# DLRM bilinear tower, head of the first chunk: pieces of weights and next indices issued at other times, landing waits of the first gathers lagged by one group

## The chip, the core and the metric

The kernel runs on one NeuronCore of a Trainium2 chip. The metric is the device time of one execution in microseconds (us). It is the median of several runs; a profile shows one execution with every instruction of every engine. The engines are TensorE (PE, with its weight loads PEld), VectorE (DVE), ScalarE (ACT), GpSimd (POOL) and SyncE (SP, which here only issues DMAs).

## What is computed

40 embedding tables are looked up for 2048 rows of a batch. Every pair of fields then gives one bilinear number, and the 780 numbers and 16 dense features go through three layers:

```python
e = jnp.stack([tbl_f[ids[:, f]] for f in range(40)], axis=1)      # (2048, 40, 64)
rowidx, colidx = pair_indices(40)                                   # 780 pairs i < j
z = jnp.einsum('bie,fie,bif->bi', e[:, rowidx], param, e[:, colidx])
h = jnp.concatenate([z, dense_ctx], axis=1)
h = jnp.maximum(h @ W_top1 + b_top1, 0.0)                           # 796 -> 512
h = jnp.maximum(h @ W_top2 + b_top2, 0.0)                           # 512 -> 256
y = h @ W_top3                                                      # 256 -> 1
```

All is float32. (`stack` and `pair_indices` are abridged here.)

## The kernel before

**Tiling.** The batch is cut into four chunks of 512 rows. Two fields make a tile, so a chunk has 20 tiles. A tile is needed in transposed form `e_t` (128 = 2 fields of 64 values, by 512 batch rows), and tiles 0 to 3 of a chunk also in the gathered form `rows` (batch rows on partitions).

**Getting a tile.** GpSimd gathers table rows with indirect DMAs (L481). One gather fetches 128 rows of one field, so a tile takes two groups of four gathers, one group for each field. TensorE then transposes the tile by four matmuls with an identity (L701), and ScalarE copies it out of PSUM into `e_t` (L502). In the first chunk only, tiles 4 to 7 (small tables) come another way: their tables are loaded whole by SyncE (L431), VectorE writes one-hots (L647), and TensorE multiplies them with the tables (L690, `look_up_tile`).

**The items.** The pairs are worked off as a list of items in a fixed order, the same for all engines. A "unit" (m, k) is two matmuls (L727) whose results VectorE multiplies into `prod` (L606, L603); sums of eight such blocks, a group, are then formed by TensorE with a strip of ones (L750, `sum_group`). VectorE may only write a slot of `prod` again (12 units) once its group is summed. A "wide" item is two matmuls (L732) for tile m against the fixed tiles 0 to 3; VectorE multiplies (L619), and ScalarE adds up the products (L541, 32 instructions each), or VectorE for some of them (L630).

**Order in the head of the first chunk.** TensorE looks up tiles 4 and 5, does the units of row 5, tile 6, the units of row 6, tile 7, the units of row 7, then transposes tiles 0 and 1, does the two units of row 1, transposes tile 2, the two units of row 2, transposes tile 3, unit (3,0), a group sum, units (3,1) to (3,3), a group sum, and from there the wide items of rows 4, 5, 6 and so on, four to a row. The transpose of tile 8 comes right before the wide items of row 6 (`TILES_AT`, items 16 and 24). Later chunks repeat the pattern without lookups, with the tiles prepared a chunk ahead.

**Weights.** The bilinear matrices come in pieces of 12 columns of 128 (768 KB), in three slots (`w`, `W_SLOTS`). SyncE issues them in one program-ordered queue: indices of chunk 0, the small tables and piece 0 between them; then it waits until tile 0 is transposed (the wait before `load_idx(1)`), issues the indices of chunk 1 and pieces 1 and 2; and from piece 3 on it waits each time until the last item that reads the piece three before is done (`t_ready`). Piece 0 holds the units of rows 5 to 7 and of rows 1 and 2, piece 1 those of row 3 and the wide items of rows 4 and 5, piece 2 the wide items of rows 6, 7 and 8. Hence piece 3 waits for row 2's last unit.

**GpSimd's queue.** It works off the tiles in the order 0 to 3, 8, 9 and so on. After each group of four gathers it waits until this group has landed, except behind the very first group. One semaphore for each slot of `rows` counts both fields. The slots are eight for the fixed tiles and six for the others. The landing wait is:

```python
if c > 0 or m > 0 or f > 0:
    pool.wait_ge(gathered[slot], 16 * BT * (f + 1 + 2 * (use - 1)))
```

TensorE's `transpose_tile` waits for the same semaphore at the count of both fields.

## Time and profile before

| what | us |
|---|---|
| median of 3 runs | 1275.88 |
| lowest and highest run | 1272.23, 1280.07 |
| profiled execution | 1274.63 |
| span of its core, first to last instruction | 1272.8 |
| TensorE busy | 1231.0 |
| VectorE busy | 1023.4 |
| ScalarE busy | 1023.9 |
| GpSimd busy | 577.7 |

The span is what the trace covers; the profiled execution's own time is 1.8 us longer. Times in the trace count from the span's start. In a row of a timeline the first number is the start, the second the length of the merged piece, and the bracket holds the idle time of the engine before it and what ended that. Busy times of matmuls overlap, since they are pipelined. "Issue" is idle time in which the engine waited for nothing that the profile shows.

### The profile page before, as it was taken

Reading aid. Unit: us, or ns where it says so; the run is one execution under the profiler, and the core shown is the slowest. Engines: PE = TensorE matmul, PEld = TensorE weight load, DVE = VectorE, ACT = ScalarE, POOL = GpSimd, SP = SyncE. Lnnn points to the kernel's source line nnn. Section 1 sums busy time; section 2 is a strip of 40 time slices with the busy share of each in tenths; the row PEclk is TensorE's granted clock in tenths of the full one; section 3 lists DMA queues with packets and bytes.
Section 4 is the critical chain, followed back from the end, with each engine's and each line's share of the span. In section 5 each row is a group of like instructions: output and inputs, shape, how many; then the busy total and the mean of one; then the engine's idle time right before and its main releaser. Section 6 shows DMA issues by size and latency. Waiting matters only on the chain.

```text
span 1272.8 us, 23705 instructions
## 1 busy us (share of the span) xinstructions
PE 1231.0 (97%) x6064; PEld 481.1 (38%) x6064; DVE 1023.4 (80%) x1680; ACT 1023.9 (80%) x7945; POOL 577.7 (45%) x615
## 2 busy tenths in 40 slices
PE   6788999999999999999999999999999999999999
PEld 3233433333333343333344333433343333343333
DVE  5768999998887777888787887788889787788980
ACT  0049988777488989998958999899968898999981
POOL 5555555555555555555345555555225554000000
PEclk9989999999999999999999999999999999999999
DMA  6311422132221222222221222122112122111100
GB/s 173 94 46 46 143 72 70 45 94 64 71 70 48 70 71 70 49 67 64 66 67 47 73 69 71 45 70 72 54 59 69 46 70 67 30 47 50 44 2 0
DMA packets 33201, 80.88 MB, mean 64 GB/s; under 512 B 11773, under 2 KB 12285, under 8 KB 32937
## 3 DMA queue, kind: packets, MB, share of 16 engines
q1 hardware_dynamic: 12320, 57.17, 13.9%
q0 software_dynamic: 19456, 19.96, 7.7%
q10 hardware_dynamic: 1288, 2.24, 0.6%
q8 instruction: 48, 0.79, 0.3%
q14 instruction: 89, 0.72, 0.2%
HBM read 79.32 MB, written 0.01 MB: 62 GB/s over the span
## 4 chain that ended last, share of the span: by engine, by line
PE 60%; ACT 31%; issue 3%; DMA 2%; POOL 2%; DVE 1%; another core or an unknown queue 1%; ACTq 0%
ACT wide_prod L541 29%; PE ring L727 26%; PE z_ps L750 13%; PE ring L732 11%; PE ring L756 7%; DMA rows<-tbl,idx_now 2%; POOL rows L481 2%; PE ring L701 2%; ACT e_t L502 1%; PE ring L760 1%; DMA idx_now<-idx 0%; DVE prod L606 0%; PE ring L763 0%; PE ring L708 0%
## 5 line engine op out<-in xcount | busy, mean ns | idle before, releaser
L541 ACT ACTIVATE wide_prod<-wide_prod 128x64 f32<-128x64 f32 x3904 | 933.7, 243 | 52.4 <-DVE wide_prod L619 25.6
L481 POOL DMA_INDIRECT rows<-tbl,idx_now x608 | 576.9, 949 | 496.7 <-DMA rows<-tbl,idx_now 292.2
L541 ACT ACTIVATION_READ_ACCUMULATOR wide_prod<-wide_prod 128x1 f32 x3904 | 739.4, 189 | 24.4 <-issue 23.4
L606 DVE TENSOR_TENSOR prod<-ring,e_t 128x512 f32<-128x512 f32 x1008 | 630.8, 683 | 147.6 <-PE ring L727 101.1
L727 PE MATMUL ring<-e_t,w 64*128 64x512 f32 x2176 | 563.0, 609 | 9.6 <-ACT e_t L502 5.9
L619 DVE TENSOR_TENSOR wide_prod<-ring,rows 128x512 f32<-128x512 f32 x512 | 328.3, 682 | 44.6 <-PE ring L732 33.3
L727 PEld LDWEIGHTS ring<-e_t,w 64*128 64x128 f32 x2176 | 215.9, 187 | 300.1 <-issue 203.7
L732 PE MATMUL ring<-w,e_t 64*128 64x512 f32 x1024 | 292.1, 607 | 11.4 <-ACT e_t L502 7.1
L750 PE MATMUL z_ps<-prod,strip 128*32 128x512 f32 x2096 | 256.2, 603 | 0.1
L732 PEld LDWEIGHTS ring<-w,e_t 64*128 64x128 f32 x1024 | 106.2, 186 | 147.0 <-issue 86.7
L750 PEld LDWEIGHTS z_ps<-prod,strip 128*32 128x32 f32 x2096 | 55.3, 109 | 182.0 <-issue 119.6
L502 ACT ACTIVATE e_t<-ring 128x512 f32<-128x512 f32 x80 | 44.7, 587 | 90.7 <-PE ring L701 47.9
L756 PE MATMUL ring<-z_t,w 128*128 128x512 f32 x224 | 99.8, 598 | 0.0
L756 PEld LDWEIGHTS ring<-z_t,w 128*128 128x128 f32 x224 | 41.4, 190 | 56.8 <-issue 49.2
L603 DVE TENSOR_TENSOR prod<-ring,e_t 64x512 f32<-64x512 f32 x80 | 54.8, 685 | 6.2 <-PE ring L727 3.9
L701 PE MATMUL ring<-ident,rows 128*128 128x128 f32 x304 | 45.5, 284 | 7.8 <-DMA rows<-tbl,idx_now 7.8
L701 PEld LDWEIGHTS ring<-ident,rows 128*128 128x128 f32 x304 | 32.5, 142 | 49.8 <-issue 41.2
L514 ACT ACTIVATE z_t<-z_ps 128x512 f32<-128x512 f32 x20 | 11.8, 588 | 38.8 <-PE z_ps L750 30.1
L690 PE MATMUL ring<-wide_prod,z_t 125*64 125x512 f32 x128 | 30.5, 631 | 10.7 <-DMA z_t<-tbl 10.7
L550 ACT ACTIVATE h<-ring,b 128x512 f32<-128x512 f32 x16 | 10.9, 683 | 27.9 <-PE ring L756 27.8
L647 DVE TENSOR_SCALAR wide_prod<-h,first_row_f 125x512 f32<-125x512 int32 x48 | 20.4, 490 | 12.1 <-DMA z_t<-tbl 8.3
L760 PE MATMUL ring<-h,w 128*128 128x512 f32 x64 | 29.2, 602 | 0.0
(23 smaller groups left out, 79.3 us busy)
## 6 DMA issues: line engine op xcount, KB each, us to landing
w<-weights SPq DMA_DIRECT2D x64, 768.0 KB
rows<-tbl,idx_now POOLq DMA_INDIRECT x608
w<-weights SPq DMA_DIRECT2D x4, 512.0 KB
z_t<-tbl SPq DMA_DIRECT2D x8, 224.0 KB
w<-w1z SPq DMA_DIRECT2D x1, 1792.0 KB
h<-hot_ids ACTq DMA_DIRECT2D x6, 256.0 KB
z_t<-hot_ids ACTq DMA_DIRECT2D x2, 256.0 KB
w<-w2p SPq DMA_DIRECT2D x1, 512.0 KB
```

Source lines behind the costliest of these rows:

```text
L481: nc.gpsimd.indirect_dma_start(out=rows[:, slot, t, E * f:E * f + E], out_offset=None, in_=tables[m * 2 + f], in_offset=bass.IndirectOffse ...
L502: nc.scalar.activation(e_t[:, m, :], ring[:, BANKS["tile", tile][0], :], ACT.Copy).then_inc(e_ready, 1)
L541: last = nc.scalar.activation(products, products, ACT.Copy, accum_out=z_b[:, h, t, col:col + 1])
L603: nc.vector.tensor_tensor(dst[half, 0, :], ring[half, bank, :], e_t[half, m - 1 + j, :], ALU.mult).then_inc(t_free, 1)
L606: nc.vector.tensor_tensor(dst[:, j, :], ring[:, bank, :], e_t[:, k, :], ALU.mult).then_inc(t_free, 1)
L619: nc.vector.tensor_tensor(dst[:, j, :, :], src[:, bank, :, :], rows[:, fixed_slot(c):fixed_slot(c) + FIXED, t, :], ALU.mult).then_inc(t_fr ...
L701: last = nc.tensor.transpose(dst[:, P * t:P * t + P], rows[:, slot, t, :], ident[:, :])
L727: nc.tensor.matmul(dst, w[field, slot, P * o:P * o + P], e_t[field, m - 1 if diagonal and b == 0 else m, :], start=True, stop=True).then_i ...
L732: nc.tensor.matmul(dst, e_t[field, m, P * t:P * t + P], w[field, slot, P * o:P * o + FIXED * P], start=True, stop=True).then_inc(t_ready, 1)
L750: last = nc.tensor.matmul(z_ps[32 * col:32 * col + 32, :], strip[:, 30 - 2 * r:62 - 2 * r], prod[:, (c * NU + UNIT_PLACE[c][u]) % PROD_SLO ...
L756: return nc.tensor.matmul(dst, w1[:, t * H1 + P * h:t * H1 + P * h + P], z_t[:, Z_NUMBER[c, t] % Z_SLOTS, :], start=start, stop=stop)
L760: return nc.tensor.matmul(dst, w2[:, k, P * h:P * h + P], h1[:, k, :], start=k == 0, stop=k == KH1 - 1)
```

## The change

Only the schedule is changed, at four places:

- SyncE issues piece 1 as soon as both fields of tile 0 have landed. Then it waits until tile 3 is transposed, issues piece 2 and after it the indices of chunk 1. Before, all three went out once tile 0 was transposed, the indices first.
- Each slot of `rows` has two semaphores, one for each field.
- For the first four tiles (the first eight groups of gathers) GpSimd waits, after it has issued a group, for the group before it. For all other tiles it waits for the group just issued, as before. The last group of tile 3 is thus waited for by nobody on GpSimd.
- TensorE waits for two semaphores instead of one before each transposed tile.

```diff
--- before.py
+++ after.py
@@ -383,7 +383,7 @@
         strip_written = sem("strip_written")
         idx_in = sem("idx_in")
         mlp_in = sem("mlp_in")
-        gathered = [sem(f"gathered{i}") for i in range(2 * FIXED + G_SLOTS)]
+        gathered = [[sem(f"gathered{i}_{f}") for f in range(2)] for i in range(2 * FIXED + G_SLOTS)]
         w_in = [sem(f"w_in{i}") for i in range(W_SLOTS)]
         dense_in = sem("dense_in")
         hot_in = [sem(f"hot_in{i}") for i in range(len(ONE_HOT))]
@@ -437,10 +437,12 @@
             for i in range(2, len(ONE_HOT)):
                 load_tables(i)
 
-            sp.wait_ge(transposed, T_NUMBER[0] + 1)
+            for f in range(2):
+                sp.wait_ge(gathered[fixed_slot(0)][f], 16 * BT)
+            load(1)
+            sp.wait_ge(transposed, T_NUMBER[FIXED - 1] + 1)
+            load(2)
             load_idx(1)
-            for piece in range(1, W_SLOTS):
-                load(piece)
             for piece in range(W_SLOTS, len(PIECES)):
 
                 sp.wait_ge(t_ready, through(PIECES[piece - W_SLOTS][2]))
@@ -463,6 +465,7 @@
                                     base=0, pattern=[[-1, P]], channel_multiplier=1).then_inc(consts, 1)
             nc.gpsimd.iota(first_row[:, :], [[1, 1]], base=0, channel_multiplier=HOT_J).then_inc(rows_known, 1)
             pool.wait_ge(idx_in, 16)
+            under_way = None
             for tile in GATHERED:
                 c, m = divmod(tile, TILES)
                 slot, use = slot_of(tile)
@@ -481,10 +484,16 @@
                         nc.gpsimd.indirect_dma_start(
                             out=rows[:, slot, t, E * f:E * f + E], out_offset=None, in_=tables[m * 2 + f],
                             in_offset=bass.IndirectOffsetOnAxis(ap=idx_now[:, c % 2, col:col + 1], axis=0),
-                        ).then_inc(gathered[slot], 16)
-                    if c > 0 or m > 0 or f > 0:
-
-                        pool.wait_ge(gathered[slot], 16 * BT * (f + 1 + 2 * (use - 1)))
+                        ).then_inc(gathered[slot][f], 16)
+                    landed = gathered[slot][f], 16 * BT * use
+                    if c == 0 and m < FIXED:
+
+                        if under_way is not None:
+                            pool.wait_ge(*under_way)
+                        under_way = landed
+                    else:
+
+                        pool.wait_ge(*landed)
 
         @block.scalar
         def _(act):
@@ -695,7 +704,8 @@
 
             def transpose_tile(tile):
                 slot, use = slot_of(tile)
-                pe.wait_ge(gathered[slot], use * 2 * BT * 16)
+                for f in range(2):
+                    pe.wait_ge(gathered[slot][f], use * BT * 16)
                 dst = take_bank(("tile", tile))
                 for t in range(BT):
                     last = nc.tensor.transpose(dst[:, P * t:P * t + P], rows[:, slot, t, :], ident[:, :])
```

## Rows read from the trace of the kernel before

**Rows 1.** The page: busy time by engine; granted clock in 40 slices of the span

```profile
PE 1231.0 (97%) x6064; PEld 481.1 (38%) x6064; DVE 1023.4 (80%) x1680; ACT 1023.9 (80%) x7945; POOL 577.7 (45%) x615
...
PEclk9989999999999999999999999999999999999999
```

**Rows 2.** Waits of TensorE, whole run: line and what it waited for, us, times, longest

```profile
PE ring L701 <- DMA rows<-tbl,idx_now: 7.8, 1, 7.8
...
PE ring L727 <- issue: 1.7, 3, 1.1
```

**Rows 3.** The chain in order of time, 60 to 84 us: start, us, what

```profile
63.18 2.44 DMA rows<-tbl,idx_now
...
80.20 3.83 ACT wide_prod L541 x31
```

**Rows 4.** The same chain, 100 to 260 us

```profile
167.18 1.13 PE ring L727 x4
```

**Rows 5.** Timeline of GpSimd: start, us, instruction, idle before and what ended it

```profile
4.92 1.11 POOL L481 DMA_INDIRECT rows<-tbl,idx_now  x1 [3.37 <-DMA idx_now<-idx]
...
14.56 1.15 POOL L481 DMA_INDIRECT rows<-tbl,idx_now  x1 [0.31 <-issue]
21.54 1.02 POOL L481 DMA_INDIRECT rows<-tbl,idx_now  x1 [5.83 <-DMA rows<-tbl,idx_now]
...
25.70 1.32 POOL L481 DMA_INDIRECT rows<-tbl,idx_now  x1 [0.30 <-issue]
28.75 0.94 POOL L481 DMA_INDIRECT rows<-tbl,idx_now  x1 [1.73 <-DMA rows<-tbl,idx_now]
...
53.05 0.94 POOL L481 DMA_INDIRECT rows<-tbl,idx_now  x1 [0.30 <-issue]
59.44 0.94 POOL L481 DMA_INDIRECT rows<-tbl,idx_now  x1 [5.45 <-DMA rows<-tbl,idx_now]
```

**Rows 6.** Timeline of SyncE's DMA issues, 50 to 60 us

```profile
51.86 6.40 SPq L421 DMA_DIRECT2D w<-weights  x3
```

**Rows 7.** The gathers' DMA queue, 4 to 15 us: packets, MB, share

```profile
q0 software_dynamic: 132, 0.14, 4.6%
```

**Rows 8.** Groups of instructions by line, GpSimd, 16 to 57.87 us

```profile
L481 POOL DMA_INDIRECT rows<-tbl,idx_now x20 | 21.1, 1055 | 17.2 <-DMA rows<-tbl,idx_now 12.6 <-issue 4.6
```

**Rows 9.** Timeline of TensorE, 50 to 90 us

```profile
54.53 0.66 PE L701 MATMUL ring<-ident,rows 128*128 128x128 f32 x4
55.88 1.99 PE L727 MATMUL ring<-e_t,w 64*128 64x512 f32 x8 [0.69 <-ACT e_t L502]
65.67 1.12 PE L701 MATMUL ring<-ident,rows 128*128 128x128 f32 x4 [7.80 <-DMA rows<-tbl,idx_now]
67.47 2.08 PE L727 MATMUL ring<-e_t,w 64*128 64x512 f32 x4 [0.69 <-ACT e_t L502]
69.47 3.64 PE L750 MATMUL z_ps<-prod,strip 128*32 128x512 f32 x16
73.05 2.89 PE L727 MATMUL ring<-e_t,w 64*128 64x512 f32 x12
75.87 1.92 PE L750 MATMUL z_ps<-prod,strip 128*32 128x512 f32 x16
77.72 3.70 PE L732 MATMUL ring<-w,e_t 64*128 64x512 f32 x16
...
87.95 2.39 PE L732 MATMUL ring<-w,e_t 64*128 64x512 f32 x7 [0.45 <-issue]
```

**Rows 10.** Stretches: us; PE, PEld, DVE, ACT, POOL busy; granted clock, DMA share, GB/s

```profile
50.00:57.87 7.87, 6.44 (x32) 2.68 (x30) 6.68 (x12) 1.68 (x3) 3.08 (x4) 1.00 0.67 224
57.87:65.67 7.80, 0.01 (x1) 0.01 (x1) 1.65 (x3) 0.00 (x0) 3.77 (x4) 0.82 0.41 121
65.67:73.05 7.38, 6.69 (x25) 1.81 (x25) 0.00 (x0) 0.60 (x1) 4.41 (x5) 0.50 0.10 20
```

**Rows 11.** Groups of instructions by line, VectorE's one-hots, 21.6 to 26.9 us

```profile
L647 DVE TENSOR_SCALAR wide_prod<-h,first_row_f 125x512 f32<-125x512 int32 x14 | 6.1, 495 | 0.0
```

## The prediction, made before the changed kernel was run

> **What bounds the kernel now.** I read the page first: TensorE is busy for 1231.0 us, 97% of the span, and only the first slices of the span show less, with the granted clock dipping in the third [rows 1]. So the body is bound by TensorE's own work, and the head is the place where time is idle. The waits of TensorE over the whole run put a number on that: one single wait of 7.80 us of the transpose at L701 for a gather's landing [rows 2]. The only longer one, before the first lookup, is untouched by this change.
>
> The chain of waits says where that stall sits. Up to 65.62 us it runs through GpSimd's gathers and their landing, then through the transposes of tile 3, units, group sums, and the first wide items; from 80.20 us it is ScalarE's reduction of the wide products [rows 3]. ScalarE sets the pace until 167 us, where the chain changes to TensorE and stays there [rows 4]. Nothing in that chain after 65.67 us waits for a transfer. Both stages are orders of instructions, written out, whose waits are on each other. If the first wide item starts x us sooner, ScalarE starts x sooner, and TensorE takes over x sooner.
>
> **Why tile 3 is late.** GpSimd issues eight groups of four gathers for tiles 0 to 3 (two fields each). It stops after every group but the first until that group has landed [rows 5]. The gathers begin at 4.92 us. Groups 1 and 2 are issued without a stop, by 14.56 + 1.15 = 15.71. Then GpSimd idles 5.83 us for group 2, behind the tables and the first piece. The usual stop is 1.7 us (1.73 before 28.75; four of this kind). The stop before the last group is 5.45 us, because its predecessor was issued up to 53.99 while SyncE's loads of pieces 1, 2 and 3 went out from 51.86 [rows 5, 6]. The last group starts at 59.44, is issued by 64.12 and has landed by 65.62 [rows 3, 5]: 1.5 us after.
>
> **The change, part by part.**
>
> *Waits lag by four gathers.* Group n+1 is issued while group n lands. At most eight gathers are open at a time, as already at the head now. When does group 3 start? Group 1 needs 4 x 32 = 128 packets of the gathers' queue, and 132 had moved by 15 us [rows 7]. So its landing is over at about 15.7, and group 3 starts near 16.0, where it now starts at 21.54. Groups 3 to 8 are 24 gathers. The 20 started between 16 and 57.87 had a mean of 1.055 us, with 0.30 between gathers [rows 8]. So 24 x 1.355 = 32.5 us: issued by 48.5, landed by 50.0. The bound on the slow side takes the longest gather of the head, 1.32 us [rows 5], for all of them, since more will now lie beside VectorE's one-hots: 24 x 1.62 = 38.9, issued by 54.9, landed by 56.4. If group 3 does not start before 21.54 but the rest holds: 21.54 + 32.5 + 1.5 = 55.5. TensorE is ready for tile 3 at 57.87 (its last unit of the row starts at 55.88 and ends 1.99 later [rows 9]). In each of these three the stall is gone; with both handicaps, 21.54 + 38.9 + 1.5 = 61.9, and 4.1 us of it stay.
>
> Tile 2 is transposed at 54.53 us, and tiles 0 and 1 before it, without a wait now, and the gathers only get earlier, so nothing is won there. The lookups before them do not use the gathers.
>
> The Trainium skill (SBUF — State Buffer, the section with the two separate sides) has a rule against this part: VectorE in a two-port mode and GpSimd hold a shared port pair exclusively, and the later one is blocked for the whole instruction. The head's longer gathers beside one-hots fit it, but no more than 1.32 - 0.94 = 0.38 us is seen of it.
>
> *Piece 1 at about 21.3 us instead of 51.9.* SyncE waits for both groups of tile 0, which end where GpSimd's wait now ends. It meets groups 3 and 4. Three pieces made one stop 5.45 - 1.7 = 3.75 us longer, so one piece costs a landing at most as much. That is 1.7 + 3.75 = 5.45 after issue, and the next group takes 4 x 1.355 = 5.4 to issue, so GpSimd waits for nothing or 0.1 us. TensorE needs piece 1 at unit (3,0), right behind tile 3: no cost. Without the cover of the lag it would be 3.75 us once, and tile 3 landed at 53.8 for 50.0, still in time.
>
> *Piece 2 and the next indices behind tile 3's transposes.* These run at about 58.5, and SyncE then issues piece 2, the indices (chunk 1's, needed beyond 200 us) and piece 3, whose condition (piece 0 read, 57.9) holds. Now three pieces, issued from 51.86, are in before 65.67, where the transfers drop to 21 GB/s [rows 6, 10]: 13.8 us at most, so all is in by 72.3. Piece 2 is first read by the wide item of row 6, at 87.95 now [rows 9] and 77.0 after: 4.7 us to spare at the least. The loads meet the gathers of tile 8, transposed just before that item; GpSimd is by then at least as far ahead of today as TensorE. The cost is nothing.
>
> *Two semaphores a slot, and one more wait before each of 76 transposed tiles.* The trace shows no such row. From below it is nothing: TensorE already waits for a bank before every matmul of a unit, more than a thousand times, and its idle time put down to issue before them is 1.7 us in all [rows 2]. From above, the gap between two gathers on GpSimd, 0.30 us [rows 5], would make 22.8 us. TensorE's own row is the nearer one: under 2 ns each, so I take 0.1 us.
>
> *The slow clock goes with the stall.* The granted clock is full from 50 to 57.87, has a mean of 0.82 in the idle stretch and is 0.50 (1.2 GHz) from 65.67 to 73.05 [rows 10]. What ran there at half rate, against its like at the full one [rows 9]: transposes and copy of tile 3 65.67 to 67.47 = 1.80 against 54.53 to 55.88 = 1.35; unit (3,0) 67.47 to 69.47 = 2.00 against a third of 73.05 to 75.87, 0.94; first group sum 69.47 to 73.05 = 3.58 against 75.87 to 77.72 = 1.85. Together 0.45 + 1.06 + 1.73 = 3.24 us. The Trainium skill (TensorE: Matmul & The Clock Gate, Part 1) has the same two levels, idle and busy; the row agrees.
>
> **Sum.** 7.80 + 3.24 - 0.1 = 10.9 us. The first wide item then starts at 57.87 + 1.35 + 0.94 + 1.85 + 2.82 + 1.85 = 66.7 instead of 77.72. The profiled execution took 1274.63 us around a span of 1272.8; it becomes 1263.7 around 1261.9. The three runs have their median 1.25 us higher, at 1275.88, so the forecast is 1275.88 - 10.9 = 1265.0, 0.85% faster.
>
> **Rivals.**
> - *Tile 3 still late.* Gathers beside one-hots grow, or the early piece delays groups 3 and 4. For it: the 5.83 us stop at 15.7 and gathers of 1.32 us; against it: room of 1.5 us or more by each single bound. With both handicaps 4.1 us stay, so 1269.1; with the clock falling too, 1272.3. A gather lengthened by one whole one-hot of 0.495 us [rows 11] each time would be 0.94 + 0.50 + 0.30 = 1.74, 24 of them 41.8, landed by 59.3, 1.4 us late: 1266.4. That is what the rule of the Trainium skill's page SBUF — State Buffer would make of it. Chance 0.10.
> - *The clock falls without the stall*, because of the short waits for ScalarE's copies there (0.69 us). Only 7.8 us come: 1268.1. Against it: 1.00 through a wait of the same 0.69 us before 55.88 [rows 9, 10]. Chance 0.05.
> - *No change.* The gain is eaten where ScalarE bounds, if something fixed in time holds the wide items: piece 2, or tile 8. Against it: the room worked out above. 1275.9. Chance 0.05.
> - *Slower.* The second wait before a transpose is not hidden, at 0.30 us for each of 76 tiles: 22.8 - 11.0, so 1287.7. It decides the sign from 11.0 / 76 = 0.145 us on. Against it: TensorE's small issue time. Chance 0.04.
> - *As forecast*: 0.76.
>
> **How the numbers follow.** A measurement of this kernel can tell about 1%, 12.8 us, from no change. The three runs before lie 7.8 us apart, so the likeliest case's own range is 1265 ± 4, 1261 to 1269. On the slow side the range takes in most of the late tile, to 1271; on the fast side a microsecond more: 1260 to 1271. Faster by over 1% needs 1263.1 or less, 1.9 us under the forecast: well within that spread, some 0.37 of the likeliest case, 0.28. Slower by over 1% is the slower rival and a little: 0.05. Within 1%: 0.67.
>
> **What would show it.** Right: GpSimd's third group starts near 16 us and the eighth is issued by 48 to 55; no wait of L701 for a gather; granted clock 1.00 from 50 to 80 us; the first wide matmul near 66.7, ScalarE's first reduction near 69.2, the change of the chain to TensorE near 156; span 1262. Piece 1 issued near 21.4, piece 2 near 58.5. Wrong: idle time of TensorE before L701 or before L732's row 6; issue gaps before transposes in the body; a stretch at 0.50 between 55 and 75 us.

## The result and the profile after

The changed kernel takes 1300.85 us in the median of six runs (1286.22 to 1303.63); the kernel before took 1274.82 beside it (six runs, 1272.23 to 1280.07). The ratio is 1.0171, with a 95% interval of 1.014 to 1.0202: slower by 1.7%, where 0.85% faster was forecast. The profiled execution is the fastest of the six, 1286.22 us around a span of 1284.4 (1272.8 before), so the trace can show only 11.6 of some 26 us.

Lines of the new kernel: gathers L484, lookups L699, transposes L711, units L737, wide items L742, group sums L760, copies into `e_t` L511, reductions L550, one-hots L656.

First the page, against [rows 1]: 9.5 us more of TensorE's busy time, and a third slice that is no better.

```profile
PE 1240.5 (97%) x6064; PEld 485.4 (38%) x6064; DVE 1023.6 (80%) x1680; ACT 1023.9 (80%) x7945; POOL 580.1 (45%) x615
...
PEclk9889999999999999999999999999999999999999
```

GpSimd's timeline, against [rows 5]. It does what the change says: the third group starts at 15.69 (before 21.54), without a stop, and the eighth, the last of tile 3, is issued by 50.20 + 0.94 = 51.14. The last landing on record for it is at 52.42; before, it had landed at 65.62 [rows 3]. The row at 55.20 is the last gather of tile 8's first group, the ninth. GpSimd does wait for that one, 1.77 us, up to 57.91.

```profile
15.69 0.94 POOL L484 DMA_INDIRECT rows<-tbl,idx_now  x1 [0.30 <-issue]
...
21.81 0.94 POOL L484 DMA_INDIRECT rows<-tbl,idx_now  x1 [1.31 <-DMA rows<-tbl,idx_now]
...
26.19 3.66 POOL L484 DMA_INDIRECT rows<-tbl,idx_now  x1 [0.30 <-issue]
...
50.20 0.94 POOL L484 DMA_INDIRECT rows<-tbl,idx_now  x1 [0.30 <-issue]
...
55.20 0.94 POOL L484 DMA_INDIRECT rows<-tbl,idx_now  x1 [0.30 <-issue]
57.91 0.94 POOL L484 DMA_INDIRECT rows<-tbl,idx_now  x1 [1.77 <-DMA rows<-tbl,idx_now]
```

TensorE's timeline, against [rows 9]. The wait of 7.80 us for a gather is gone: tile 3 is transposed at 77.61 with no idle time before it. But there is a new wait of 9.59 us, put down to issue, before the units of row 7. The first wide item starts at 86.52; before it was 77.72, and 66.7 was forecast.

```profile
46.46 2.50 PE L699 MATMUL ring<-wide_prod,z_t 125*64 125x512 f32 x6 [0.34 <-issue]
50.21 1.07 PE L699 MATMUL ring<-wide_prod,z_t 125*64 125x512 f32 x2 [1.24 <-DVE wide_prod L656]
60.87 5.27 PE L737 MATMUL ring<-e_t,w 64*128 64x512 f32 x16 [9.59 <-issue]
...
69.60 2.56 PE L737 MATMUL ring<-e_t,w 64*128 64x512 f32 x8 [2.44 <-issue]
...
77.61 0.69 PE L711 MATMUL ring<-ident,rows 128*128 128x128 f32 x4
...
86.52 3.70 PE L742 MATMUL ring<-w,e_t 64*128 64x512 f32 x16
```

What do the units of row 7 wait for? ScalarE's copy of tile 7. Its row in ScalarE's timeline, and two rows of the waits of the whole run (us, times, longest):

```profile
60.22 0.60 ACT L511 ACTIVATE e_t<-ring 128x512 f32<-128x512 f32 x1 [21.86 <-remote]
```

```profile
ACT wide_prod L550 <- issue: 47.0, 106, 1.0
ACT e_t L511 <- remote: 46.9, 6, 21.9
```

TensorE's last matmul of tile 7 had ended at 51.28 us, ScalarE was idle, and the copy starts 8.9 us later. "Remote" says that the profile finds no instruction ending when the semaphore rose. The trace also records when each semaphore is incremented. Here the one that TensorE increments at the end of matmuls which read a one-hot (VectorE's one-hots wait for it), and the one for a finished tile:

```
changed kernel, us from the span's start
 matmuls ended     41.40 41.40 42.26 42.26 43.11 43.12 43.97 43.98 44.83 44.84 45.69 46.12 47.53 47.93 48.97
 increments        41.62       43.04 43.09 44.48       45.90 45.94 47.33 49.46 50.20 52.36 55.23 57.34 58.74 58.78 59.46
 tile 7: ended 51.28, increment 60.19
kernel before
 matmuls ended     40.41 40.42 41.27 41.28 42.13 42.13 42.99 42.99 43.84 43.85 44.70 44.71 45.56 45.57 46.42
 increments        40.43 40.47 41.28 41.33 42.14 42.19 43.00 43.04 43.86 43.90 44.72 44.76 45.58 45.62 46.43
```

Before, every increment is there 0.01 to 0.06 us after its matmul. Now they trail further and further, by 2 us at 48 and 10 at 59 (some increments are not recorded one by one). At first one, or two at once, come each 1.4 us, where the matmuls end in pairs 0.86 us apart. Nothing in the program had touched them: increments sent by TensorE arrive late while GpSimd issues gather after gather. They are slowed, not stopped, and a stop does not let them all out: in GpSimd's stop from 56.14 to 57.91 a single one comes.

In TensorE's start times against those before, matmul by matmul, this makes +4.4 us by 50 us and +13.7 at 60.9. The clock is at half in two stretches, one around the wait of 9.59 us and one behind the wait of 2.44 us (windows: PE, PEld, DVE, ACT, POOL busy; clock; DMA share; GB/s):

```profile
53.80:64.10 10.30, 3.23 (x8) 1.53 (x10) 1.12 (x2) 0.60 (x1) 5.67 (x6) 0.50 0.13 23
...
70.90:77.70 6.80, 6.11 (x17) 1.99 (x14) 3.81 (x6) 0.60 (x1) 4.25 (x5) 0.50 0.09 19
```

With them it is +18.5 at 74.9 and +19.3 at the last unit of row 2, at 76.6. Then the old stall and its slow clock fall out, 10.5 us in all. The wide items start with +8.8, and the end comes at +11.6.

### The profile page after: what moved, and what is told of

Read it like the earlier page. It is cut to its first block, busy times and chain, and to the rows that moved or that the text cites. A ratio compares the mean times of both kernels' runs of the same rounds, so it can differ in the third digit from the quotient of the medians.

```text
span 1284.4 us, 23706 instructions
## 1 busy us (share of the span) xinstructions
PE 1240.5 (97%) x6064; PEld 485.4 (38%) x6064; DVE 1023.6 (80%) x1680; ACT 1023.9 (80%) x7945; POOL 580.1 (45%) x615
## 4 chain that ended last, share of the span: by engine, by line
PE 81%; ACT 13%; issue 3%; DVE 1%; DMA 1%; another core or an unknown queue 1%; SPq 0%; ACTq 0%; DVEq 0%
PE ring L737 35%; PE z_ps L760 17%; PE ring L742 15%; ACT wide_prod L550 12%; PE ring L766 7%; PE ring L711 2%; PE ring L770 2%; PE ring L699 2%; DVE prod L615 1%; ACT e_t L511 1%; DMA z_t<-tbl 1%; PE ring L773 0%; PE ring L718 0%; DVE wide_prod L628 0%
## 5 line engine op out<-in xcount | busy, mean ns | idle before, releaser
L550 ACT ACTIVATE wide_prod<-wide_prod 128x64 f32<-128x64 f32 x3904 | 933.6, 242 | 53.1 <-issue 24.9
L484 POOL DMA_INDIRECT rows<-tbl,idx_now x608 | 579.3, 953 | 503.2 <-DMA rows<-tbl,idx_now 275.0
L550 ACT ACTIVATION_READ_ACCUMULATOR wide_prod<-wide_prod 128x1 f32 x3904 | 736.7, 189 | 22.7 <-issue 22.2
L737 PE MATMUL ring<-e_t,w 64*128 64x512 f32 x2176 | 570.4, 611 | 22.3 <-issue 13.7
L737 PEld LDWEIGHTS ring<-e_t,w 64*128 64x128 f32 x2176 | 218.5, 187 | 316.8 <-issue 209.3
L742 PE MATMUL ring<-w,e_t 64*128 64x512 f32 x1024 | 295.2, 606 | 6.7 <-DVE wide_prod L628 2.7
L760 PE MATMUL z_ps<-prod,strip 128*32 128x512 f32 x2096 | 253.9, 598 | 0.0
L742 PEld LDWEIGHTS ring<-w,e_t 64*128 64x128 f32 x1024 | 108.3, 186 | 142.4 <-issue 86.6
L511 ACT ACTIVATE e_t<-ring 128x512 f32<-128x512 f32 x80 | 44.8, 586 | 106.6 <-remote 46.9
L760 PEld LDWEIGHTS z_ps<-prod,strip 128*32 128x32 f32 x2096 | 55.0, 109 | 179.1 <-issue 114.7
L711 PEld LDWEIGHTS ring<-ident,rows 128*128 128x128 f32 x304 | 32.6, 142 | 43.3 <-issue 43.3
L699 PE MATMUL ring<-wide_prod,z_t 125*64 125x512 f32 x128 | 33.3, 640 | 12.7 <-issue 11.4
L711 PE MATMUL ring<-ident,rows 128*128 128x128 f32 x304 | 45.5, 285 | 0.0
L559 ACT ACTIVATE h<-ring,b 128x512 f32<-128x512 f32 x16 | 10.9, 680 | 26.3 <-PE ring L766 26.1
L656 DVE TENSOR_SCALAR wide_prod<-h,first_row_f 125x512 f32<-125x512 int32 x48 | 20.6, 494 | 13.0 <-DMA z_t<-tbl 8.5
```

The lines of the kernel that those rows point to most:

```text
L484: nc.gpsimd.indirect_dma_start(out=rows[:, slot, t, E * f:E * f + E], out_offset=None, in_=tables[m * 2 + f], in_offset=bass.IndirectOffse ...
L511: nc.scalar.activation(e_t[:, m, :], ring[:, BANKS["tile", tile][0], :], ACT.Copy).then_inc(e_ready, 1)
L550: last = nc.scalar.activation(products, products, ACT.Copy, accum_out=z_b[:, h, t, col:col + 1])
L699: last = nc.tensor.matmul(dst[E * h:E * h + E, :], hot_table[2 * i + h][:, E * j:E * j + E], hot[number % len(hot)], start=j == 0, stop=j ...
L711: last = nc.tensor.transpose(dst[:, P * t:P * t + P], rows[:, slot, t, :], ident[:, :])
L737: nc.tensor.matmul(dst, w[field, slot, P * o:P * o + P], e_t[field, m - 1 if diagonal and b == 0 else m, :], start=True, stop=True).then_i ...
```

## Experiments

All ratios are to the kernel before, run on the same chip beside it. A line "Measured" gives the kernel's median in us, the median of the kernel before where it is the first of its chip, then the ratio and in brackets its 95% interval. The edits shown are shortened to the lines that matter.

### Which part does it?

`e1_again` is the changed kernel, unchanged. `e1_lag` has the two semaphores and the lag, with SyncE's queue as before. `e1_sp` has the two semaphores and SyncE's new queue, with the landing waits as before. `e1_sems` has the semaphores alone. Against the changed kernel:

```diff
# e1_lag: SyncE as before
-            for f in range(2):
-                sp.wait_ge(gathered[fixed_slot(0)][f], 16 * BT)
-            load(1)
-            sp.wait_ge(transposed, T_NUMBER[FIXED - 1] + 1)
-            load(2)
+            sp.wait_ge(transposed, T_NUMBER[0] + 1)
             load_idx(1)
+            for piece in range(1, W_SLOTS):
+                load(piece)
# e1_sp: no lag
-                    if c == 0 and m < FIXED:
-
-                        if under_way is not None:
-                            pool.wait_ge(*under_way)
-                        under_way = landed
-                    else:
+                    if c > 0 or m > 0 or f > 0:
```

> The changed kernel as it is, once more. All theories expect 1286 to 1304 us again, as its six executions so far. The question is what its trace looks like in an execution near 1300 us: theory M (increments of TensorE's semaphores arrive late while GpSimd keeps up to eight gathers open) expects more or longer stretches like the one from 51.3 to 60.2 us, where the transposed tile 7 was announced 8.9 us after TensorE's last matmul, and all of them before some 60 us, while the lag lasts. Theory B (the body itself is slower, for a cause that has nothing to do with the head) expects the head like the one seen and 15 us more behind 100 us.

Measured: 1235.94 against 1247.29, ratio 0.9933 (0.9909 to 0.9958).

> Two semaphores a slot and the lagged landing waits, but SyncE's queue as before. Theory M: the lag alone does it, so the loss is all here: 1286 to 1305 us, lookups with late increments between 16 and 60 us. Theory P (the early load of piece 1, or SyncE's wait for a gather's semaphore, does it): about 1264 us, as was forecast for the whole change, or up to 1268 with the three pieces meeting the gathers. Theory S (two semaphores and the second wait): slow here too, 1286 or more.

Measured: 1233.09, 0.9909 (0.9877 to 0.9941).

> Two semaphores a slot and SyncE's queue as in the change, but the landing waits as before. Theory M: no late increments; the stop of 5.45 us before the last group becomes 1.7, one earlier stop grows by up to that much, so tile 3 comes 0 to 3.75 us sooner: 1271 to 1276 us. Theory P: slow, 1286 or more. Theory S: slow, 1286 or more.

Measured: 1246.83, 1.0012 (0.9994 to 1.0031).

> Only the second semaphore of each slot and TensorE's second wait before a transposed tile; SyncE's queue and the landing waits as before. Theories M and P: no difference to the kernel before, 1272 to 1278 us. Theory S: all the loss is here, 1286 to 1304 us, with 0.15 to 0.4 us for each of 76 transposes, or late increments in the head without any lag.

Measured: 1247.55, 1.0003 (0.9977 to 1.0029).

This was another chip than the first, and on it the same two kernels came out the other way round: 1247 for the kernel before and not 1275, and the change faster, not slower. Four chips of this study ran the kernel before at 1247 to 1249 us (the first kind below); the first chip and three more at 1264 to 1275 (the second kind). Only one chip was measured twice, 15 minutes apart, and it was of the first kind both times. So "kind of chip" is the reading that fits; a state that a chip passes through is not excluded.

On the first kind the forecast mechanism is there. TensorE's timeline of `e1_sems`, then of `e1_again`:

```profile
55.60 1.99 PE L730 MATMUL ring<-e_t,w 64*128 64x512 f32 x8 [0.69 <-ACT e_t L504]
64.57 1.09 PE L704 MATMUL ring<-ident,rows 128*128 128x128 f32 x4 [6.98 <-issue]
...
76.83 3.70 PE L735 MATMUL ring<-w,e_t 64*128 64x512 f32 x16
...
354.83 0.66 PE L704 MATMUL ring<-ident,rows 128*128 128x128 f32 x4
367.63 1.09 PE L704 MATMUL ring<-ident,rows 128*128 128x128 f32 x4 [12.14 <-issue]
```

```profile
56.07 1.99 PE L737 MATMUL ring<-e_t,w 64*128 64x512 f32 x8 [0.69 <-ACT e_t L511]
57.99 0.66 PE L711 MATMUL ring<-ident,rows 128*128 128x128 f32 x4
...
66.87 3.70 PE L742 MATMUL ring<-w,e_t 64*128 64x512 f32 x16
...
345.05 0.66 PE L711 MATMUL ring<-ident,rows 128*128 128x128 f32 x4
351.79 1.09 PE L711 MATMUL ring<-ident,rows 128*128 128x128 f32 x4 [6.09 <-issue]
```

The stall of 6.98 us is gone, the clock is 1.00 from 50 to 80 us, and the first wide item starts at 66.87, 9.96 us earlier (66.7 was forecast). The rows near 350 us show what was not forecast: TensorE catches up with GpSimd there and waits 12.14 us for a tile of the second chunk. With GpSimd ahead from the head on, by 15.3 us at the start of the eighth group (43.11 against 58.38), 6.09 remain, so the whole gain at the end of these two traces is 16.1 us. SyncE's part and the second semaphore are worth nothing that can be measured; on this kind the lag is all of it.

### Does the half clock cost what the rows said, and is GpSimd the bound at 350 us?

`e4_filler` is the kernel before with eight more matmuls (their result is overwritten) in the stall before tile 3. They stand before the wait for the gathers, and so does the wait for the tile's bank now. This keeps the stall and takes the slow clock away. `e4_lag` repeats `e1_lag` beside it.

```diff
+                dst = take_bank(("tile", tile))
+                if tile == FIXED - 1:
+                    for _ in range(FILLERS):
+                        nc.tensor.matmul(dst, ident[:, :], e_t[:, 0, :], start=True, stop=True)
                 pe.wait_ge(gathered[slot], use * 2 * BT * 16)
-                dst = take_bank(("tile", tile))
```

> The kernel before, with eight more matmuls (identity by a tile, 128 columns by 512, 0.86 us each, 6.9 us in all, results overwritten) put on TensorE in the stall before tile 3's transposes, so that it waits without being idle. Theory C (the stretch at half clock comes from the idle time): the granted clock stays full, tile 3 is not sooner, and 2.6 us are won, as much as the offset between the traces of the change and of the kernel with only two semaphores grew behind the stall: ratio 0.998. Rival: the clock falls anyway or the extra matmuls reach beyond the landing: no gain, ratio 1.000 to 1.001. What it does not win of the change's gain is the stall itself.

Measured: 1249.12 against 1248.59, 1.0012 (0.9993 to 1.0032).

> Two semaphores a slot and the lagged waits, SyncE's queue as before, with more rounds. Where the kernel before takes 1247 us: if SyncE's part is worth nothing once the waits lag, a ratio of 0.988 to 0.991, as the change itself had on three jobs (0.9933, 0.9894, 0.9876); if it is worth the collision's 3.75 us, 0.991 to 0.994. Where the kernel before takes 1275 us: 1.015 or more if the lag is the trigger of the late increments, 0.992 if it is SyncE's part.

Measured: 1232.81, 0.9885 (0.9853 to 0.9916).

Two rows of windows, first 64.57 to 71.90 us of `e1_sems`, then the stall of `e4_filler` (PE, PEld, DVE, ACT, POOL busy; clock; DMA share; GB/s), and the rows of its TensorE that show where the gain went:

```profile
64.57:71.90 7.33, 6.64 (x24) 1.79 (x24) 0.00 (x0) 0.60 (x1) 4.60 (x5) 0.50 0.10 20
```

```profile
57.50:64.70 7.20, 7.14 (x18) 2.96 (x16) 1.73 (x3) 0.00 (x0) 3.77 (x4) 1.00 0.43 129
```

```profile
73.61 3.70 PE L736 MATMUL ring<-w,e_t 64*128 64x512 f32 x16
...
361.31 0.66 PE L705 MATMUL ring<-ident,rows 128*128 128x128 f32 x4
368.28 1.09 PE L705 MATMUL ring<-ident,rows 128*128 128x128 f32 x4 [6.32 <-DMA rows<-tbl,idx_now]
```

With the clock kept at full, the first wide item starts at 73.61 and not at 76.83: 3.22 us, where the prediction had 3.24. None of it reaches the end. The tile that TensorE needs next at 350 us is there at 368.28 against 367.63, whatever TensorE did in the head: GpSimd had not been moved. On this kind of chip only what brings GpSimd forward brings the end forward.

### More lag, on the first kind

`e2_lagall` is the change with the lag for every tile; `e3_lagall_only` has that lag with SyncE's queue as before; `e2_lag8` waits for the group before the last (twelve gathers open) in the first four tiles. `e2_again` and `e3_again` are the changed kernel beside them.

```diff
# e2_lagall
-                    if c == 0 and m < FIXED:
-
-                        if under_way is not None:
-                            pool.wait_ge(*under_way)
-                        under_way = landed
-                    else:
-
-                        pool.wait_ge(*landed)
+                    if under_way is not None:
+                        pool.wait_ge(*under_way)
+                    under_way = landed
# e2_lag8
-                        if under_way is not None:
-                            pool.wait_ge(*under_way)
-                        under_way = landed
+                        if under_way is not None and len(under_way) == 2:
+                            pool.wait_ge(*under_way.pop(0))
+                        under_way = (under_way or []) + [landed]
```

> The changed kernel once more. Two chips have given two answers: 1275 us before and 1301 after on the first, 1247 before and 1236 after on the second. Theory K (it is the chip): on a chip where the kernel before takes about 1275 us, and where ScalarE's reductions show gaps of 0.3 to 1 us after each landing of gathers, the change costs some 20 us, through late increments in the head; on a chip at about 1247 us, without these gaps, it gains 11 us. Theory N (it was a passing state of the first chip or job): the gain is there whatever the kernel before takes.

Measured: 1232.78 against 1247.25, 0.9894 (0.9854 to 0.9934).

> The changed kernel with the lagged landing wait for every tile, not only the first four. On a chip at 1247 us before: the last stall of TensorE for a gather (6.1 us at 346 to 352 us in the trace of the change, 12.1 before) goes with its stretch at half clock, so 8 us more than the change: about 1228 us; if that stall is not GpSimd's lateness but a transfer's own time, 1236 as the change. On a chip at 1275 us before, theory K with late increments for as long as eight gathers are open: far slower, 1330 us or more, since it lasts for the whole run; theory N: about 1255.

Measured: 1224.38, 0.9831 (0.9789 to 0.9874).

> The changed kernel with the landing wait of the first four tiles lagged by eight gathers, so up to twelve open. On a chip at 1247 us before: tile 3 was in time already with a lag of four, only the stop of 0.5 us at 20.9 goes, so 1236 as the change, and at most 1 us better at tile 28. On a chip at 1275 us before, theory K: the more gathers are open, the later the increments, so slower than the change by some us, 1305 to 1315; if the number open does not matter, 1301.

Measured: 1231.94, 0.9895 (0.9853 to 0.9938).

> The changed kernel on whatever chip comes. Theory K: about 1235 us where the kernel before takes 1247 and its trace keeps all 16 landing increments of each gather; about 1300 us where the kernel before takes 1275 and increments are missing from the trace, with TensorE's increments in the head late. Theory N: a gain of some 11 us in either case.

Measured: 1232.78 against 1249.37, 0.9876 (0.9855 to 0.9897).

> Landing waits lagged by four gathers for every tile, SyncE's queue as in the kernel before. If the moved loads of pieces 1 and 2 bring nothing of the gain: 1224 us at 1247 before, as with them. If they do bring something once the waits lag, the three pieces meeting the gathers at 52 us cost a part of the head's gain: 1228 us. On a chip with 1275 us before, theory K and the lag as its trigger: slower than the change, over 1310 us; if it is SyncE's part that triggers it, under 1265.

Measured: 1224.63, 0.9809 (0.9788 to 0.983).

Lag by one group is enough in the head; the lag everywhere takes the rest of the stall at 350 us too (in `e2_lagall` the pair of transposes runs at 345.14 without a wait) and gives the two fastest kernels here, 1.7 to 1.9% faster than the one before. So far this reads as a success.

### The second kind: one stop less, SyncE's queue, and the lag with a pause

`e5_pairs` (SyncE as before) issues both groups of a tile and then waits for both: eight gathers open as with the lag, but GpSimd stops after each eight. `e5_sp` is `e1_sp`. `e6_lag` is `e1_lag`. `e6_breath` is `e1_lag` with four small memsets on GpSimd after each group of the first four tiles, each waited for, a pause of 1.8 to 2.4 us from the end of a group to the next gather.

```diff
# e5_pairs
-                        if under_way is not None:
-                            pool.wait_ge(*under_way)
-                        under_way = landed
+                        if f == 1:
+                            pool.wait_ge(gathered[slot][0], 16 * BT)
+                            pool.wait_ge(*landed)
# e6_breath
+                        for _ in range(BREATHS):
+                            breaths += 1
+                            nc.gpsimd.memset(scratch[:, :], 0.0).then_inc(breath, 1)
+                            pool.wait_ge(breath, breaths)
                         if under_way is not None:
```

> Two semaphores a slot, SyncE's queue as before; for the first four tiles GpSimd waits once a tile, for both its fields, instead of once a field. So up to eight gathers open as with the lag, but four stops. Theory G (at 1247 us before: the end goes by GpSimd's time, since TensorE waits for it again near 350 us): the stops after the first field of tiles 1 to 3 go, of 1.7, 1.7 and 1.7 us or a little more, so GpSimd is 5 to 6 us earlier, TensorE's stall near 350 us is 5 to 6 us shorter, ratio 0.995 to 0.997. Theory T (the end goes by TensorE's head alone): the head's stall of 7.0 us shrinks by the same 5 and the clock may stay: 0.993. Where the kernel before takes 1275 us: if more than four open gathers are the trigger of the late increments, 1.01 or more; if it is GpSimd never waiting, 0.995.

Measured: 1269.25 against 1273.38, 0.9978 (0.9953 to 1.0003).

> SyncE's queue as in the change, two semaphores a slot, landing waits as before, as once already (ratio 1.0012, 0.9994 to 1.0031). Where the kernel before takes 1247 us: the same, 1.000 to 1.003. Where it takes 1275 us: 1.015 or more if SyncE's part is the trigger of the loss there, about 1.000 if the lag is.

Measured: 1273.50, 1.0011 (0.9991 to 1.0032).

> Two semaphores a slot and the lagged waits, SyncE's queue as before. Where the kernel before takes 1273 to 1275 us and its trace has gaps in ScalarE's reductions (the slow kind of chip; SyncE's part alone gave 1.0011 there): theory K with the lag as the trigger says 1.013 to 1.02 and late increments of TensorE in the head; if it takes lag and moved loads together, 0.99 to 0.995. Where the kernel before takes 1247 us: 0.9885 to 0.991 once more.

Measured: 1269.33 (1256.35 to 1278.32) against 1263.73, 1.0022 (0.9988 to 1.0055).

> The lag without SyncE's part, and after each of the first eight groups four small memsets on GpSimd, each waited for: a pause of 1 to 3 us without any gather's landing being waited for. On the fast kind: theory G says that GpSimd's time is the end's time, so eight pauses cost the 8 to 20 us that GpSimd loses, up to the point where tile 3 is late again; the eighth group would be issued by 56 to 68 instead of 54.5 us, and the ratio is 0.995 to 1.003 instead of 0.989. On the slow kind: if gathers without a pause are what holds TensorE's increments back, they are in time again and the ratio is 0.99 to 1.00; if it is that no landing is waited for, it stays at 1.015.

Measured: 1264.08, 1.0008 (0.9989 to 1.0028). The eighth group is issued by 61.61 us here and by 48.51 in `e1_lag`; the 54.5 of the expectation is near the end of the ninth there.

`e5_sp` clears SyncE's part alone here too. TensorE's timeline of `e6_lag` and then of `e6_breath`:

```profile
29.96 7.09 PE L697 MATMUL ring<-wide_prod,z_t 125*64 125x512 f32 x32
43.59 3.78 PE L735 MATMUL ring<-e_t,w 64*128 64x512 f32 x8 [6.55 <-issue]
...
64.83 6.35 PE L735 MATMUL ring<-e_t,w 64*128 64x512 f32 x16 [3.16 <-issue]
...
87.01 3.27 PE L740 MATMUL ring<-w,e_t 64*128 64x512 f32 x14
```

```profile
37.76 1.99 PE L743 MATMUL ring<-e_t,w 64*128 64x512 f32 x8 [0.72 <-ACT e_t L517]
...
47.48 3.70 PE L743 MATMUL ring<-e_t,w 64*128 64x512 f32 x16 [0.72 <-issue]
...
75.00 3.70 PE L748 MATMUL ring<-w,e_t 64*128 64x512 f32 x16
```

ScalarE's copies of tiles 6 and 7 in `e6_lag`, then its copy of tile 2 in `e5_pairs`:

```profile
42.94 0.60 ACT L509 ACTIVATE e_t<-ring 128x512 f32<-128x512 f32 x1 [14.96 <-remote]
64.18 0.60 ACT L509 ACTIVATE e_t<-ring 128x512 f32<-128x512 f32 x1 [20.64 <-remote]
```

```profile
57.12 0.60 ACT L509 ACTIVATE e_t<-ring 128x512 f32<-128x512 f32 x1 [4.73 <-remote]
```

The lag alone brings the late increments back, without SyncE's part: the copies of tiles 6 and 7 start 5.9 and 2.5 us after everything they need has ended (37.04 and 61.67 us), and the first wide item is at 87.01. The same kernel on the first kind had no late copy. With the pause no copy in the head is late, at the same eight open gathers, and the first wide item is 12 us earlier. In `e5_pairs` one copy in the head is 2.1 us late. So it is not the number of open gathers.

Is it the missing stops, or only the faster pace of the gathers? `e6_breath` does not tell: its 24 gathers of groups 3 to 8 take 42.5 us from start to end, as long as in the kernel before (42.6). `e5_pairs` does in part: 35.0 us, the pace of the changed kernel (35.5), with a stop after each eight gathers, and its latest copy is 2.1 us late and not 8.9. That speaks for the stops, over two chips and one trace of each.

In time the lag alone did not do what either theory said: 1.0022, where the lag as the only trigger was to cost 1.3 to 2%. On this chip it was even with the kernel before, although its first wide item is as late as the changed kernel's. It is 12.0 us behind `e6_breath` there and 7.3 at the end of the traces, and in the ratios the two cannot be told apart. The changed kernel was 1.7% slower on the first chip. How much of that is the lag's alone, how much needs SyncE's loads beside it, and how much is the chip or the single execution, no run separates.

`e7_breath1`, with one memset a group, was to find the smallest pause that helps, beside `e7_again`, the changed kernel. The chip turned out to be of the first kind, so it could only say that the small pause costs nothing there.

> The changed kernel on whatever chip comes, after one chip (8, 11, 5) kind at 1247 us and three at 1264 to 1275. Where the kernel before takes 1260 us or more: ratio 1.002 to 1.02, with late increments of TensorE between 16 and 65 us in the trace, as on the first chip and as the lag alone showed at 1264. Where it takes 1247: 0.988 to 0.993, none late.

Measured: 1233.58 against 1248.50, 0.9906 (0.9876 to 0.9937).

> The lag without SyncE's part, with one small memset of GpSimd a group instead of four: a pause of some 0.8 instead of 2.4 us. Where the kernel before takes 1260 us or more: if any pause lets the held increments out, they are in time, tile 3 lands near 57 us and the ratio is 0.990 to 0.997; if the length of the pause matters, some are late and it is 1.000 or more. Where it takes 1247 us: theory G, GpSimd 8 x 0.5 us later than with the lag alone: ratio 0.991 to 0.994.

Measured: 1233.77, 0.9892 (0.9858 to 0.9926).

### The dose: the lag for every tile, on the second kind

`e8_lagall_only` is `e3_lagall_only`, to the letter. If gathers issued back to back are the cause, then more of them must hold TensorE back more.

> The lag of four gathers for every tile, SyncE's order as before; on chips of the first kind it ran at 0.981 of the kernel before. Theory A (gathers issued back to back, with no stop of GpSimd, hold back TensorE's increments, but only on a chip of the second kind, on which the kernel before takes 1264 to 1275 us): on such a chip TensorE's copies of tiles 6 and 7 are 3 us late or more in the head, TensorE is behind by 10 us at 70 us, and further late increments show wherever GpSimd runs without a stop in the body; ratio 1.00 to 1.04. Rival B (the loss in the head does not matter, since on either kind the end is set by GpSimd near 350 us): ratio 0.98 to 0.985 on either kind. If the chip is of the first kind (before at 1247), both say 0.981 again, and the second kind stays open for this kernel.

Measured: 1800.60 us (1792.63 to 1805.35) against 1275.35, ratio 1.4134 (1.4093 to 1.4174). One of the two fastest kernels of the first kind is by 41% the slowest of the second. Theory A has the direction right, and its own number, 1.00 to 1.04, is far too small. GpSimd's, TensorE's, ScalarE's and VectorE's timelines of `e8_lagall_only`, and the windows 48 to 88 us and the last 180 us:

```profile
55.68 0.95 POOL L482 DMA_INDIRECT rows<-tbl,idx_now  x1 [0.30 <-issue]
56.94 0.95 POOL L482 DMA_INDIRECT rows<-tbl,idx_now  x1 [0.30 <-issue]
```

```profile
47.08 1.59 PE L692 MATMUL ring<-wide_prod,z_t 125*64 125x512 f32 x2 [1.04 <-issue]
87.90 3.79 PE L730 MATMUL ring<-e_t,w 64*128 64x512 f32 x8 [39.23 <-issue]
```

```profile
87.24 0.60 ACT L504 ACTIVATE e_t<-ring 128x512 f32<-128x512 f32 x1 [55.84 <-remote]
```

```profile
76.05 0.49 DVE L649 TENSOR_SCALAR wide_prod<-z_t,first_row_f 125x512 f32<-125x512 int32 x1 [5.11 <-remote]
81.65 0.49 DVE L649 TENSOR_SCALAR wide_prod<-z_t,first_row_f 125x512 f32<-125x512 int32 x1 [5.11 <-remote]
```

```profile
48.00:88.00 40.00, 0.77 (x3) 0.11 (x2) 5.62 (x11) 0.60 (x1) 30.36 (x32) 0.50 0.15 27
1610.00:1790.00 180.00, 178.60 (x838) 68.34 (x830) 125.77 (x207) 144.06 (x1125) 0.00 (x0) 1.00 0.09 30
```

For 40 us the core does little but gather: 32 gathers, one each 1.25 us, 11 instructions of VectorE, and TensorE idle at the half clock. The transfers are at 15% of the DMA engines, so these are not full. TensorE's increments come out one at a time, from 65 us on one each 5.60 us, and tile 6's behind those of the one-hots that were read before it:

```
                       matmul ended   increment
 tile 6 finished
   e8_lagall_only         48.67         87.22
   e3_lagall_only         46.52         46.57    (the same kernel, first kind)
 one-hot read, e8_lagall_only: matmuls ended by 46.04; increments 50.77 55.02 ... 64.82 70.42 76.02 81.62
```

It stays so for as long as there are gathers. TensorE's start times, the same kernel on the two kinds, by number of the matmul:

```
 matmul       0   200   800   2200   3600   4600   5200   5600   6000
 first      10.5  60.7 189.7  452.4  722.8  916.2 1036.3 1116.7 1192.9
 second     10.7 136.0 340.9  762.9 1175.5 1417.9 1604.3 1684.7 1760.9
 behind      0.2  75.3 151.2  310.5  452.7  501.7  568.0  568.0  568.0
```

The last gather ends at 1564.5 us. From there on TensorE loses nothing more and is busy 178.6 of 180 us, at full clock. 568.0 us over 608 gathers are 0.93 us a gather. And in the body it is the stretches with gathers that lose: between matmuls 200 and 400 it gives up 8 us with 23 gathers, between 600 and 800 it gives up 51 with 51. In the list of waits TensorE and GpSimd now hold each other up:

```profile
POOL rows L482 <- PE ring L704: 799.0, 40, 56.4
ACT wide_prod L543 <- issue: 339.5, 480, 10.5
```

The second row is ScalarE, inside a reduction that waits for nothing: 480 gaps. The changed kernel has 106 of them (its row stands above), the kernel before 100 on the first chip, the first kind none. The third mark of the second kind is in the records of landings. Sixteen increments for each of 608 gathers make 9728. On the first kind the trace has 9694 to 9707 (`e1_lag`, `e1_again`, `e1_sems`), 9593 in `e3_lagall_only`. On the second it has 4411 in the kernel before, 4144 in the changed one, 4251 in `e6_lag`, 1749 in `e8_lagall_only`. Whether they are not made singly or only not recorded the trace doesn't say; they are fewest where the increments of TensorE are latest. (The Trainium skill, DMA: Bandwidth & Descriptors, section Why a DMA increments its semaphore by 16 and not by 1, has all sixteen engines post one each for such a gather; the first kind's records agree.)

## Why the prediction was wrong

**Tile 3's stall, 7.80 us [rows 2].** Right as far as it goes: the third group starts at 15.69 (16.0 forecast), the eighth is issued by 51.14 (48.5, at most 54.9 forecast), and L711 waits for no gather. The 24 gathers of groups 3 to 8 took 35.5 us from start to end, 1.48 each, where 1.355 was put in and 1.62 was the upper bound. On the first kind (`e1_again`) they took 32.6 us, issued by 48.11, and the stall that went was 6.98 us.

**The slow clock (3.24 us).** The size was right, 3.22 us by the filler on the first kind. On the first chip the half clock came back, 53.8 to 64.1 and 70.9 to 77.7 us, around and behind waits that were not there before. "Granted clock 1.00 from 50 to 80 us" was wrong there (0.72) and right on the first kind.

**SyncE's queue and the second wait (nothing, 0.1 us).** Right where the landing waits are as before: 1.0012 and 1.0011 on either kind, and 1.0003 (0.9977 to 1.0029) for the semaphores alone on the first, which excludes the bound of 22.8 us. Beside the lag it is right on the first kind (`e1_lag` against `e1_again`); on the second that pair was not run on one chip.

**"At most eight gathers are open at a time, as already at the head now."** This is the step that failed. It priced the removed stops as idle time of GpSimd alone, and asked only what gathers cost gathers. But the stops gave something to all engines: on this kind of chip the increments of TensorE come late where GpSimd issues gathers without the stops, and in time where it has them. The kernel before never issues more than eight gathers without a stop; the changed one issues 36, from 4.59 to 56.14 us, with one stop of 1.31 us. The price on the first chip was +19.3 us in TensorE's start times by 77 us, against the 10.5 us won back. No row of the trace of before prices that, since its increments in the head are all in time. A sign of something was there, though, in ScalarE's waits in the trace of before:

```profile
ACT wide_prod L541 <- issue: 46.8, 100, 1.0
```

These are gaps inside reductions that wait for nothing. About half of those of 0.3 to 1.3 us (68 of 139) begin 0.25 to 0.85 us after the end of the fourth gather of a group. That is in GpSimd's stop, while the group lands, so they do not say whether issuing or landing is what reaches the other engines.

**"Both stages shift as a whole."** Near the truth for the loss on the first chip (+8.8 us at the first wide item, +11.6 at the end). Not true of the gain on the first kind: there the end is set by a meeting of TensorE and GpSimd at 350 us, so that 9.96 us in the head became 16.1, and the filler's 3.22 us became nothing. The medians gained 11.4 to 16.6 us in the four runs of the changed kernel on this kind, against 10.9 forecast. The head came out as forecast; that 11.4 at the end is so near is luck, since the sum has no term for the meeting at 350 us.

**The rivals.** The slower result is not the slower rival's: the second wait costs nothing. Nor was tile 3 late: one gather in the head reached 3.66 us, so 1.32 was no bound for a single gather, but the tile was in time. The clock did not fall by the short waits for ScalarE's copies alone: it is 1.00 through them in `e1_again`. (By the rule of SBUF — State Buffer in the Trainium skill, as the prediction worked it out, the 24 gathers were to take 41.8 us and tile 3 to be late; they took 35.5, and the trace does not bear that out.)

**Shown and open.** Shown: on the first kind the lag is the whole gain. On the second kind the lag delays the increments that TensorE sends, in every trace that has it without a pause (the changed kernel, `e6_lag`, `e8_lagall_only`); with a pause after each group they are in time in the head; and with the lag for every tile the loss is 41%. Not shown: what in the chip delays the increments, whether GpSimd's issuing, its pace or the landings do it, whether it is the chip or a state of it, why the loss differs between executions (1286 to 1304, 1256 to 1273), and the smallest pause that is enough. Nor is it shown that the lag alone makes the 1.7% of the changed kernel, which was measured on one chip of the second kind only. (The Trainium skill, VectorE: DVE Perf Modes, in its section The TRN2 errata, warns that increments at a high rate from one engine can deadlock another, and tells to space them. Here nothing hangs, and no run ties its mechanism to this one; `e6_breath` spaced the gathers, and with them their landings.)

A kernel clearly better than before on both kinds was not found. On the second kind `e5_pairs` (0.9978, 0.9953 to 1.0003) and the pause (1.0008) are at least even, but neither was measured on the first. The kernel before is the safe one.

## What to carry to other kernels

A wait that seems to cost only its own engine's idle time may be what keeps others in time: before you take out a stop between indirect DMAs, look at who sends semaphore increments meanwhile, and compare the time of the increment with the end of the instruction that makes it. "Remote" in the waits, where one core runs alone, was the sign here. Measure such a change on several chips; here one chip says 1.9% faster and the next 41% slower, for the same program. And ask of a gain in the head what meets it next: if the bound changes hands to an engine that you did not move, the gain ends there.

## What was not expected of the hardware

- Two kinds of chip: the kernel before takes 1247 to 1249 us on four and 1264 to 1275 on four, with the same program. The traces from the slower ones have the gaps in ScalarE's reductions (42 to 480 of them) and more than half of the landing increments missing from the records.
- A semaphore increment of TensorE 38.5 us late, the ones before it released one each 5.60 us, while GpSimd issues a gather each 1.25 us.
- On the one chip where it was run, a pause of GpSimd of 1.8 to 2.4 us for each four gathers was enough to have none late in the head.
- Eight matmuls in a stall of 7 us held the clock at 1.00; without them it was 0.84 in the stall and 0.50, the lower level of 1.2 GHz, for 7.3 us of work behind it.
